# Reordering the last two steps of the first phase of a two-layer graph attention kernel

## The reference

```python
# layer 0, applied to relu(layernorm(x)), result added to x
h = x @ W
e = leaky_relu((h @ a1)[:, None] + (h @ a2)[None, :], 0.2)
x = x0 + elu(softmax(where(adj > 0, e, -9e15), axis=1) @ h)
# layer 1, applied to relu(layernorm(x)), result added to x
q, k, v = x @ Wq.T + bq, x @ Wk.T + bk, x @ Wv.T + bv
s = where(adj > 0, q @ k.T / sqrt(128), -9e15)
x = x + elu(softmax(s, axis=-1) @ v)
```

## Time and profile before

| | |
|---|---|
| three runs | 1686.07, 1687.95, 1689.50 us (median 1687.95) |
| the profiled execution | 1688.92 us, of which its span (first to last instruction) is 1687.2 us |
| mean granted TensorE clock | 0.696 of full speed |
| busy time | PE 1204.0 us (71%), DVE 1189.1 us (70%), POOL 1132.0 us (67%), ACT 938.6 us (56%) |
| HBM | 353.80 MB read, 12.72 MB written |

### The profile page before, as it was taken

The page is one execution under the profiler, slowest core; times in us unless marked ns, Lnnn a source line. Parts: engine busy times, 40 slices in busy tenths (PEclk is TensorE's granted clock), DMA queues, the critical chain, the costliest instruction groups (busy, mean ns, idle before and its releaser), DMA issues.

```text
span 1687.2 us, 23399 instructions
## 1 busy us (share of the span) xinstructions
PE 1204.0 (71%) x5503; PEld 952.4 (56%) x5554; DVE 1189.1 (70%) x6433; ACT 938.6 (56%) x1955; POOL 1132.0 (67%) x1206
## 2 busy tenths in 40 slices
PE   2657887777877777877766476776777777776765
PEld 1344555555555555655546365666666666666664
DVE  3557899888888888888887355655665565566555
ACT  2769888888888888888853233223323332332322
POOL 1237777667666666666675577777777777777773
PEclk9778777777777777777765566666566556556655
DMA  9869999999999999999922122222222222222221
GB/s 287 342 223 393 397 399 398 400 400 400 399 397 388 384 382 381 388 384 393 359 62 55 52 59 66 62 61 65 65 64 65 64 66 63 64 66 64 66 66 40
DMA packets 113048, 368.10 MB, mean 218 GB/s; under 512 B 33553, under 2 KB 58642, under 8 KB 80146
## 3 DMA queue, kind: packets, MB, share of 16 engines
q1 hardware_dynamic: 66242, 285.50, 43.6%
q0 software_dynamic: 38464, 81.08, 17.2%
q10 hardware_dynamic: 8208, 0.03, 0.3%
HBM read 353.80 MB, written 12.72 MB: 217 GB/s over the span
## 4 chain that ended last, share of the span: by engine, by line
POOL 34%; DMA 31%; issue 13%; DVE 9%; PE 7%; ACT 5%; SPq 1%; POOLq 0%; ACTq 0%; DVEq 0%
POOL arena L596 33%; DMA arena<-in_adj_dram 29%; ACT arena L1158 4%; PE psum L1370 2%; DMA table<-arena 1%; PE psum L1431 1%; DVE arena L860 1%; POOL arena L567 1%; PE psum L1403 1%; SPq L452 1%; PE psum L1417 1%; DVE arena L653 1%; DVE arena L693 0%; DVE arena L755 0%; DVE arena L752 0%
## 5 line engine op out<-in xcount | busy, mean ns | idle before, releaser
L567 POOL DMA_INDIRECT arena<-table,arena x576 | 552.4, 959 | 246.5 <-issue 162.2
L596 POOL DMA_INDIRECT arena<-table,arena x576 | 551.2, 957 | 184.0 <-issue 184.0
L1158 ACT ACTIVATE arena<-arena 128x2048 bf16<-128x2048 int32 x256 | 486.9, 1902 | 98.1 <-DMA arena<-in_adj_dram 97.4
L1370 PE MATMUL psum<-arena 128*128 128x512 bf16 x973 | 283.1, 430 | 56.8 <-ACT arena L1158 51.1
L860 DVE SCALAR_TENSOR_TENSOR arena<-arena 128x131 f32<-128x131 f32 (+1 forms) x768 | 266.3, 347 | 15.2
L1417 PE MATMUL psum<-arena 128*128 128x131 f32 (+1 forms) x768 | 200.6, 433 | 103.9 <-ACT arena L1305 102.2
L1403 PE MATMUL psum<-arena 128*128 128x18 f32 x768 | 142.8, 318 | 148.2 <-DVE arena L823 147.8
L1417 PEld LDWEIGHTS psum<-arena 128*128 128x128 f32 x768 | 179.5, 329 | 107.6 <-issue 107.6
L1403 PEld LDWEIGHTS psum<-arena 128*128 128x128 f32 x768 | 136.2, 261 | 166.7 <-DVE arena L823 166.4
L1370 PEld LDWEIGHTS psum<-arena 128*128 128x128 bf16 x1024 | 111.3, 117 | 192.3 <-issue 70.5
L1410 PE MATMUL psum<-arena 128*128 128x1 f32 x768 | 140.7, 299 | 96.1 <-DVE arena L843 96.1
(11 more groups left out here) (203 smaller groups left out, 2067.9 us busy)
## 6 DMA issues: line engine op xcount, KB each, us to landing
arena<-in_adj_dram SPq DMA_DIRECT2D x256, 1024.0 KB, 22.4
arena<-table,arena POOLq DMA_INDIRECT x1152
table<-arena POOLq DMA_DIRECT2D x32, 132.0 KB, 3.5
table<-arena SPq DMA_DIRECT2D x16, 256.0 KB
arena<-table SPq DMA_DIRECT2D x64, 64.0 KB, 1.9
out_dram<-arena SPq DMA_DIRECT2D x16, 256.0 KB, 2.4
arena<-in_x_dram SPq DMA_DIRECT2D x4, 0.5 KB, 12.4
arena<-in_L_gnn_W_dram SPq DMA_DIRECT2D x1, 64.0 KB
```

The source lines that it names most:

```text
L567: pool.indirect_dma_start(Gt[:, v % GROUP, c + 1, :], None, table0, bass.IndirectOffsetOnAxis(idx_all[:, v, c:c + 1], 0))\
L596: pool.indirect_dma_start(Gt[:, t % GROUP, c + 1, 0:D], None, table1, bass.IndirectOffsetOnAxis(idx_all[:, t, c:c + 1], 0))\
L1158: nc.scalar.activation(mask[:, k, q * QUARTER:(q + 1) * QUARTER], adj_sb[:, k, q, :], ACT.Relu, accum_out=sum_all[:, bass.ds(tile, 1), q:q ...
L1370: nc.tensor.matmul(V[k], shifted[:, s, :], mask[:, k, s * 512:(s + 1) * 512], start=(s == 0), stop=False)
```

## The change

Three edits, all in the first phase; nothing that is computed changes.

1. In steps 68 and 69 (`ahead = t > T + PICK`) DVE does the whole of tile w (`weigh`, slots, `total`, `finish`, `measure`) first, and `score0(u)` and `maxima(u)` after it. In place of `score0`'s wait at the head of the step stands a wait for `self_done` of u.
2. PE in those steps takes `sum_up(w)` ahead of `scatter(u)`, and ACT takes `post(w)` ahead of `prob_rows(u)`.
3. In step 69, for the last tile (63), slots 0 to 3 are added right behind `maxima` (after a wait for `prob_rows`), and step 70 adds slots 4 to 6 only (EARLY = 4).

```diff
--- before.py
+++ after.py
@@ -408,6 +408,7 @@
 
         PICK, LATE, DONE = 3, 6, 7
         NORM, TURN = 4, 5
+        EARLY = 4
         PAIRS = T // 2
         UNITS = T // 2
 
@@ -931,24 +932,37 @@
                     if live(t, -1):
                         at_least(dve, packed, t)
                         hide_diag(t + 1, (b + 1) % 2)
-                    if live(t, LATE):
+                    ahead = t > T + PICK
+                    if live(t, LATE) and not ahead:
                         score0(u, u % 2, u % GROUP, u // GROUP + 1)
                     if live(t, DONE):
                         weigh(w, w % 2, w % GROUP)
                     if live(t, PICK):
                         mark(v, v % GROUP)
+                    if live(t, LATE) and ahead:
+                        dve.wait_ge(self_done, u + 1)
 
                     for n in range(PARTS):
-                        if n == 0 and live(t, DONE):
+                        if n == 0 and live(t, DONE) and w < T - 1:
                             add_self(w, w % 2)
-                        elif n < OWN and live(t, DONE):
+                        elif n < OWN and live(t, DONE) and (w < T - 1 or n >= EARLY):
                             add_slot(w, w % 2, w % GROUP, n, D + 3)
                         if live(t, 0):
                             extract(t, b, n)
-                    if live(t, LATE):
+                    if live(t, LATE) and not ahead:
                         maxima(u, u % 2)
                     if live(t, DONE):
                         total(w, w % 2, D + 3)
+                    if live(t, LATE) and ahead:
+                        finish(w, w, w % 2)
+                        measure(w, w % GROUP)
+                        score0(u, u % 2, u % GROUP, u // GROUP + 1)
+                        maxima(u, u % 2)
+                    if u == T - 1:
+                        dve.wait_ge(p_done, 2 * u + 1)
+                        add_self(u, u % 2)
+                        for n in range(1, EARLY):
+                            add_slot(u, u % 2, u % GROUP, n, D + 3)
                     if t < 3:
                         for i in range(12 * t, min(12 * t + 12, UNITS)):
                             keep_turned(i)
@@ -965,7 +979,7 @@
                         list_tile(t - 1, pair)
                         if b % 2 == 0:
                             count(t - 2, (t - 2) % GROUP, pair)
-                    if live(t, DONE):
+                    if live(t, DONE) and not (live(t, LATE) and ahead):
                         finish(w, w, w % 2)
                         measure(w, w % GROUP)
                     if live(t, LATE):
@@ -1215,10 +1229,13 @@
                     if live(t, PICK):
                         act.wait_ge(deal_done, v + 1)
                         nc.scalar.activation(owned_list[:, v % GROUP, :, :], deal_ps[v % 2], ACT.Identity).then_inc(owned_done, 1)
-                    if live(t, LATE):
+                    ahead = t > T + PICK
+                    if live(t, LATE) and not ahead:
                         prob_rows(u, u % 2)
                     if live(t, DONE):
                         post(w, w % 2, acc_sb[:, w % 2, 0:D])
+                    if live(t, LATE) and ahead:
+                        prob_rows(u, u % 2)
                     if live(t, NORM):
                         o = t - NORM
                         at_least(act, self_turned, o - GROUP + 1)
@@ -1434,6 +1452,8 @@
                     if live(t, DONE):
                         at_least(pe, summed, w - 1)
                         sum_up(w, w % 2, w % GROUP, D + 3)
+                    if live(t, LATE) and ahead:
+                        scatter(u, u % 2, u % GROUP)
                     if live(t, TURN):
                         o = t - TURN
                         pe.wait_ge(self_h_done, o + 1)
```

## The result

The changed kernel takes 1693.04 us (median of 9 runs, 1689.47 to 1695.04) against 1687.16 us (median of 9): a ratio of 1.0031 with a 95% interval of 1.0021 to 1.0041, or 5.2 us more, between 3.5 and 6.9. (The ratio is not the quotient of the two medians, which lie 5.9 us apart.) Forecast: 4.9 us more, 1692.9.

What follows compares the result with a forecast made beforehand. POOL's second-phase gathers, without slack, were taken to pass on any delay of DVE's steps 68 to 70. 7.45 us lost less 2.5 given back is +4.9: 1687.95 + 4.9 = 1692.9 us, range 1688.5 to 1695.0.

Steps and rivals of the forecast that it cites:

- The second phase has no slack, so what moves its first gather moves the end: POOL's 576 second-phase gathers wait for nothing but issue, so the end shifts by as much as the first gather.
- first gather at about 944: Sign in the profile after: POOL's second phase starts at about 944 us; at or before 941 the forecast is wrong.
- Block A: DVE's run from a tile's sums to its statistics and the next independent instruction, L853 to L889: 5.46 us.
- Block B: DVE's run from scores to `below`: 4.36 us, about 2.9 of it standing still for PE's scatter and `spread_max`.
- Scores of tile 63 7.45 us later: On DVE in step 69, the last tile's scores start at 927.14 instead of 919.69 us, with no wait for rows.
- The moved wait costs nothing: DVE's wait for `self_done` at L867: PE's own product is ready at 921.88, wanted at 922.15 us.
- From scores to total 7.59: The last tile takes 7.59 us from its scores to its total, against 10.10 before.
- This part gives back 2.5 us: Part two, the early slots of tile 63: from scores to total the last tile gets 2.5 us shorter.
- PE at half speed: PE's durations priced at a granted clock of 0.50, 1.2 GHz, as over 905 to 930 us before.
- The rival of a faster clock: PE's exposed work in these steps runs at twice the speed: only +1.9 us, 1689.8; chance 0.08.
- Only the idle stretch counts: DVE's 1.67 us wait for rows in step 69 is won back, bared work hidden: -1.67 us, 1686.3; chance 0.07.
- The rows late: Tile 63's rows land at least 5.0 us later, so not slower; gain 2.5 us at most, 1685.4; chance 0.03.

Runs made afterwards that it cites:

- the run of step 68 alone: Changed kernel with the sums ahead of the scores in step 68 only and no early slots: 1689.76 us, ratio 1.0013 to the kernel before.
- The order alone: Changed kernel without early slots, sums still ahead of scores in steps 68 and 69: 1692.81 us, ratio 1.0030 to the kernel before.
- weave only: Kernel before, with weigh, add_self and slot 1 of tile 62 ahead of tile 63's scores, PE's sum_up ahead of scatter there: 1684.87 us, ratio 0.9987.
- the delayed pairs: Kernel before and changed kernel, each with extra gathers ahead of tile 63's: two, 1692.29 and 1691.90 us; four, 1699.36 and 1695.40 us.
- the woven kernel: Changed kernel, but step 68 in old order, only part of tile 62's sums ahead of scores, finish cut in two: 1684.40 us, ratio 0.9982.

## Why the prediction was right

The mechanism held, term by term: bared PE legs, scores 7.5 us later, 2.7 us given back. That the median came out within 0.2 us of the forecast is luck: the kernel before has a median of 1687.16 us in nine runs, 0.8 below the 1687.95 that I started from, and the two medians differ by 5.9 us and not 4.9. The sum itself is borne out by the stretch, +4.80 us.

- **The second phase has no slack, so what moves its first gather moves the end**: held. Gap of total to first gather 9.30 for 9.26; 723.7 us from first to last gather, the idle time again all issue. I had named 725 as the mark; the true scatter of this number is about 2 us, which I didn't know from one profile. The same goes for the mark "first gather at about 944": it stood at 941.62, because the step began 2.27 us sooner, and so came within 0.7 us of the 941 that I had named as a sign of being wrong. Absolute positions in one execution were poor marks; the stretch was a good one.
- **Block A 5.46 us**: measured 5.46 twice. **Block B 4.36 us**: measured 4.36. The 0.04 us for a return from PE, an estimate from another engine's pair, is what the rows show (L1420 ends, by the profile's modelled end, at 915.55 + 1.47 = 917.02, L842 starts at 917.06).
- **From `below` to the sums 0.42**: 0.43. **Scores of tile 63 7.45 us later**: 7.46 (15.71 against 8.25).
- **The moved wait costs nothing**: held in the change. But the same product is waited for where no `weigh` stands in front, 0.56 us in the run of step 68 alone.
- **From scores to total 7.59**: 7.44; `below` came 0.16 sooner (4.62 us after the scores, for 4.78), since it starts 1.05 us after the first of the three additions and not 1.20.
- **"This part gives back 2.5 us", said of the early slots**: the size holds for the two parts together (10.10 to 7.44), the name doesn't. The order alone already brings it to 8.04, since with no sums between scores and maxima the last tile's way is shorter; the early slots add 0.60 in the new order and 0.29 in the old. The sum is not touched by it, but who had kept only the early slots by my text would have hoped for 2.5 us and got 0.3.
- **PE at half speed**: the window from 905 to 930 us has a granted clock of 0.50 again, with PE busy for 12.2 us. The rival of a faster clock, +1.9 us, fell. (Its sum takes PE's last leg at half, 0.82 us less, but DVE's own slots end 0.72 us before that leg did, so by the same rows it would have been +2.0.) The Trainium skill (TensorE: Matmul & The Clock Gate, section on the clock gate) and the trace agree here, as far as a clock that never rose can show it.
- **Only the idle stretch counts**, -1.67 us: fell as the outcome of this change. The gap did close, but waits for PE opened: 3.0 us in step 68, and in step 69 1.49 us (3.0 without the early slots). Filling the gap with the cover kept, as weave only does, brings 1.24 us from scores to total. By the section Optimization Strategy of Perfetto Trace Analysis in the Trainium skill, a gap is the place to look; the trace agrees for weave only, not for the whole change.
- **The rows late**: the place where the sign turns was put at 5.0 us of delay. From the measured parts it is 23.15 - 10.10 = 13.05 us into the stretch, 4.8 later than before; the delayed pairs lie on the far side of it, with 1.4 and 2.0 us of gain in the stretch (0.7 and 2.7, had the rows of each pair landed at the same point).

Not tried: whether DVE's wait for `post` (0.84 us in each step) can be filled in step 68 too, and what the early slots bring in the woven kernel without the cut finish.

## What to carry to other kernels

When work that is ready is moved ahead of work that waits, look at what it covered where it stood. Here 3 us of sums hid one PE leg of 1.5 us, and the total and finish behind them hid a second; moving all of that to fill a gap of 1.67 us opened gaps of up to 3.0 us a step and put the last tile's scores 7.5 us back; moving just what the gap holds gained. And for a change in one place of a long kernel, compare the stretch between two fixed instructions in both profiles: from the scores of tile 63 to its total it was 10.10 to 10.12 us in four runs of the old order, while times of the kernel before ran from 1682.9 to 1691.7 us.

## What the runs showed that I had not expected

A gather with a wait for its own landing costs 2.7 to 2.9 us on POOL, about 0.95 of issue and 1.8 to 1.9 of wait, in eleven of the twelve extra gathers of the delayed kernels; one took 3.65 us. The start of step 68 differs by over 5 us between executions of the same code, and the 576 gathers of the second phase take 723.0 to 725.5 us from first to last; together these are larger than the effect that was looked for.
